# A graph network on one core: low halves of the first node stage computed by GpSimd instead of VectorE

## The chip, the cores and the metric

The kernel runs on one core of one Trainium2 chip. The metric is the time of one execution on the device in microseconds (us). Each run was taken three times; the median is compared. The engines have these names in the profile: PE is TensorE (matmuls), PEld its weight loads, DVE is VectorE, ACT is ScalarE, POOL is GpSimd, SP is SyncE, whose queue here only issues DMAs.

## What is computed

Four graph layers over N = 6250 nodes of 128 features and E = 106250 edges, each followed by a residual and a layernorm:

```python
x = _layernorm(x + _L0_gnn_ref(x, ...))   # relu(relu((x + sum of neighbours) @ W1.T + b1) @ W2.T + b2)
x = _layernorm(x + _L1_gnn_ref(x, ...))   # 4 GCN convolutions: dinv * sum over edges of dinv * h[src], W1..W4
x = _layernorm(x + _L2_gnn_ref(...))      # convolution with edge features
x = _layernorm(x + _L3_gnn_ref(...))      # 2 SAGE convolutions
```

The change concerns the end of the first layer: the layernorm of the first line, and the preparation of its result as operand of the first GCN convolution.

## The kernel before

The sums over neighbours are matmuls with a dense matrix of edge counts ("adjacency"), held in fp8 in HBM. The node features are the stationary operand (128x128, f16). To keep float32 accuracy, each feature block is used as two f16 halves: with a scale c, **high** = f16(c*x) and **low** = f16(c*x - high). Both halves are multiplied with the same adjacency piece and added up in PSUM.

The node features `XN` are 128 partitions x 6272 columns of float32, 49 blocks of 128 nodes. The first node stage goes over them in NQ = 7 chunks (`q` = 0 to 6) of QB = 7 blocks (896 columns). For each chunk:

1. PE: `hidden_0` (L1843), ACT: `relu_0` (L1509), PE: second weight, giving `Y0` in PSUM (L1856).
2. DVE `rows_0(q)`: adds the bias (L1103), takes relu and adds to `XN` (L1105), row statistics (L1108, L1111, L1114).
3. ACT `root_0(q)` (L1515), then DVE `factors_0(q)`: reciprocal (L1119) and the tiny product `c2 = -mean * 1/deviation` (L1121, 128x7, both inputs in SBUF). ScalarE waits for `c2`.
4. ACT `high_0(q)`: normalises `XN` in place, block by block (L1521), then writes the high half `HI[1]` (L1525, tile HN); raises `s_hi`.
5. DVE `low_0(q)`: the low half `LO[1]` (second half of tile HN), seven instructions of 128 columns (L1129), since the scale `c1[:, b]` is one number for each partition and block; raises `s_split`.

DVE runs rows_0(q), factors_0(q-1), low_0(q-2) in that order; ACT runs root_0(q), relu_0(q+2), high_0(q). PE begins the next pass in between: `piece(n)` multiplies seven blocks with two 250-column parts of the adjacency (28 matmuls of 500 columns for a pair of pieces, L1707). Pieces 2j and 2j+1 need the two halves of chunk j, hence `s_split` at NQ + j + 1. Pieces 0 to 7 follow the rows of chunks 3 to 6; pieces 8 to 13 (chunks 4, 5, 6) come behind all rows.

After the stage DVE goes on with `hot(0)` (L1313), the sums of pass 1 (L1203), and the chain `lengths`, `bounds` (L1146 to L773), on which the scales of later passes hang. GpSimd, until then idle, waits for all of `s_split` and adds a bias to `XN` in seven instructions of 896 columns (`bias_1`, L719); that is first read in pass 4. Later it weights edge features (L751).

A tile matters here: `AGN` holds the float32 sums' f16 halves of the input (`HI[0]`, `LO[0]`) until the last sub pass, and is free in the node stage; the first pass writes its results into it.

Of the kernel before, what the change touches and what calls it, by code (L numbers as in the profile page):

```python
# [4 lines left out]
P = 128  # L5


def build(nc, a, out):
# [5 lines left out]
    ALU = mybir.AluOpType  # L14
# [16 lines left out]
    QB = 7  # L31
    NQ = NB // QB
    QN = QB * P
# [86 lines left out]
    with ExitStack() as ctx:  # L120
        def sb(name, shape, dt=fp32):
            return ctx.enter_context(nc.sbuf_tensor(name, shape, dt))

        def sem(name):
            return ctx.enter_context(nc.semaphore(name))

        XN = sb("XN", [P, NP])
        HN = sb("HN", [P, NP])
        HR = sb("HR", [P, NP])
        AGN = sb("AGN", [P, NP])  # L130
# [26 lines left out]
        c1 = sb("c1", [P, NB])  # L157
# [12 lines left out]
        HI = [t[:, 0:NP // 2].bitcast(f16) for t in HL]  # L170
        LO = [t[:, NP // 2:NP].bitcast(f16) for t in HL]
# [178 lines left out]
        s_hi, s_split = sem("high_ready"), sem("split_ready")  # L350
# [280 lines left out]
        def _(pool):  # L631
            g_ = nc.gpsimd
# [64 lines left out]
            def general(p):  # L697
                pool.wait_ge(s_tab, 32 * (PASSES.index(p) + 1))

                def tile(g, j, t, n):  # L700
                    pool.wait_ge(s_stage, NT * PASSES.index(p) + t + 1)
                    pool.sem_inc(s_scrap, 1)
                    g_.indirect_dma_start(out=msg, out_offset=None, in_=Hd[:, :],
                                          in_offset=bass.IndirectOffsetOnAxis(ap=si[:, 0:1], axis=0)).then_inc(s_g[p], 16)
                    g_.indirect_dma_start(out=old, out_offset=None, in_=Gd[:, :],
                                          in_offset=bass.IndirectOffsetOnAxis(ap=di[:, 0:1], axis=0)).then_inc(s_old[p], 16)
                    pool.wait_ge(s_new, NT * PASSES.index(p) + t + 1)
                    pool.sem_inc(s_scrap, 1)
                    g_.indirect_dma_start(out=Gd[:, :], out_offset=bass.IndirectOffsetOnAxis(ap=xi[:, 0:1], axis=0),
                                          in_=new, in_offset=None, bounds_check=NP - 1,  # L710
                                          oob_is_err=False).then_inc(scattered(p, 0)[0], 16)

                tiles(pool, tile)

            def residual_bias(k):

                with pool.Fori(0, NQ) as q:
                    x = XN[:, ds(q * QN, QN)].rearrange("p (b f) -> p b f", f=P)
                    g_.tensor_tensor(x, x, BR[:, k, :].unsqueeze(1).to_broadcast([P, QB, P]), ALU.add)  # L719
                pool.drain().then_inc(s_res, 1)  # L720

            def bias_1():

                pool.wait_ge(s_split, 2 * NQ)
                residual_bias(1)

            def bias_5():

                pool.wait_ge(s_split, splits(5, NU - 1))
                pool.wait_ge(s_tb, idx(5, NU - 1) + 1)  # L730
                residual_bias(5)

            with pool.If(flags["pool"]):
                pool.wait_ge(s_un, NS_)
                g_.memset(at, 0.0)
                g_.affine_select(out=low, in_=ones[:, :], compare_op=ALU.is_gt, fill=0.0, base=0,
                                 pattern=[[-1, P]], channel_multiplier=1)
                pool.drain().then_inc(s_low, 1)
                for p in PASSES:
                    if p == 1:  # L740
                        bias_1()
                    if p == 6:
                        bias_5()
                    general(p)
            with pool.Else():

                def weighted(g):

                    e3 = AE[g % 2].rearrange("p (j f) -> p j f", j=J)
                    pool.wait_ge(s_aem, g + 1)  # L750
                    g_.tensor_tensor(e3, e3, NS[:, g * J:(g + 1) * J].unsqueeze(2).to_broadcast([P, J, DE]), ALU.mult).then_inc(s_aes, 1)  # L751

                bias_1()
                pool.wait_ge(s_ns, 1)
                for g in range(NG):
                    weighted(g)
                bias_5()
        @block.vector
        def _(dve):
            v = nc.vector  # L760
# [314 lines left out]
            with dve.If(flags["dve"]):  # L1075
# [10 lines left out]
                for q in range(NQ):  # L1086
                    cols = slice(q * QN, (q + 1) * QN)
# [11 lines left out]
            def rows_0(q):  # L1099
                cols = slice(q * QN, (q + 1) * QN)  # L1100
                y = Y0[q % 2]
                dve.wait_ge(s_y0, q + 1)
                v.tensor_tensor(three(y), three(y), bias(0, QB), ALU.add)  # L1103
                dve.drain()
                v.scalar_tensor_tensor(out=XN[:, cols], in0=y, scalar=0.0, in1=XN[:, cols], op0=ALU.max, op1=ALU.add).then_inc(s_yb0, 1)  # L1105
                dve.drain()
                for b in range(q * QB, (q + 1) * QB):
                    v.bn_stats(ST[:, b, :], XN[:, b * P:(b + 1) * P])  # L1108
                dve.drain()
                for b in range(q * QB, (q + 1) * QB):  # L1110
                    v.bn_aggr(MV[:, b, :], ST[:, b, :])  # L1111
                dve.drain()
                bs = slice(q * QB, (q + 1) * QB)
                v.tensor_scalar(VE[:, bs], MV[:, bs, 1], EPS, None, ALU.add).then_inc(s_var0, 1)  # L1114
# [6 lines left out]
                v.scalar_tensor_tensor(out=c2[:, bs], in0=MV[:, bs, 0], scalar=-1.0, in1=RS[:, bs],  # L1121
                                       op0=ALU.mult, op1=ALU.mult).then_inc(s_nr0, 1)

            def low_0(q):
                for b in range(q * QB, (q + 1) * QB):
                    cols = slice(b * P, (b + 1) * P)
                    if b == q * QB:
                        dve.wait_ge(s_hi, NQ + q + 1)
                    last = v.scalar_tensor_tensor(out=LO[1][:, cols], in0=XN[:, cols], scalar=c1[:, b:b + 1], in1=HI[1][:, cols],  # L1129
                                                  op0=ALU.mult, op1=ALU.subtract)  # L1130
                last.then_inc(s_split, 1)

            dve.wait_ge(s_aw[0], 16 * len(range(0, NS_, 3)))
            v.tensor_scalar(c1[:, :], dinv[:, :], SC[:, 1, 0:1], None, ALU.mult)
            for q in range(NQ + 2):
                if q < NQ:
                    rows_0(q)
                if 0 < q <= NQ:
                    factors_0(q - 1)
                if q > 1:  # L1140
                    low_0(q - 2)


            def lengths():
# [10 lines left out]
            def bounds():  # L1155
                dve.wait_ge(s_nrt, 1)
                v.scalar_tensor_tensor(out=BND[:, 2:3], in0=NRT[:, 4:5], scalar=LNB, in1=NRT[:, 7:8], op0=ALU.mult, op1=ALU.add)
                v.scalar_tensor_tensor(out=BND[:, 5:6], in0=NRT[:, 3:4], scalar=LNB, in1=BND[:, 5:6], op0=ALU.mult, op1=ALU.add)
                v.tensor_tensor(BND[:, 0:1], NRT[:, 5:6], NRT[:, 6:7], ALU.add)
                dve.drain()  # L1160
                v.scalar_tensor_tensor(out=BND[:, 7:8], in0=BND[:, 0:1], scalar=LNB, in1=BND[:, 7:8], op0=ALU.mult, op1=ALU.add)
                v.scalar_tensor_tensor(out=BND[:, 2:3], in0=BND[:, 2:3], scalar=1.001, in1=NRT[:, 0:1], op0=ALU.mult, op1=ALU.mult)
                dve.drain()
                for p in (2, 5, 7):
                    scale_of(p, BND[:, p:p + 1])
                dve.drain().then_inc(s_scale, 1)
# [212 lines left out]
            with dve.If(flags["dve"]):  # L1379
                for p in range(1, LASTP + 1):  # L1380
                    if p == 1:
                        lengths()
                        bounds()
                    dve.drain()
                    v.tensor_tensor(HR[:, :], HI[p % 2], LO[p % 2], ALU.add)
                    dve.drain()
                    v.tensor_scalar(HR[:, :], HR[:, :], SC[:, p, 1:2], UNIT, ALU.mult, ALU.mult).then_inc(s_gh, 1)
                    if p in (2, 3):
                        for i in (3, 4, 5):
                            measure_steps(p, i)  # L1390
                    general(p)
                    for u in range(NU):
                        general_sums(p, u)
                        rows_read(p, u)
                        if p in LAG["norm"]:
                            normalise(p, u)
                        if p == 4:
                            second(p, u)
                        if p < LASTP:
                            low_half(p, u)  # L1400
            with dve.Else():
                hot(0)
                for n in range(ALL + TAIL):
                    p, i = n // PCS + 1, n % PCS
# [661 lines left out]
```

## Time and profile before

| | |
|---|---|
| median of 3 runs | 2577.36 us (2572.64 to 2578.82) |
| time of the profiled execution | 2576.27 us |
| its span | 2574.4 us, mean granted TensorE clock 0.992 |
| PE busy | 2472.4 us (96%) |
| DVE busy | 1308.8 us (51%) |
| ACT busy | 599.7 us (23%) |
| POOL busy | 162.3 us (6%) |

The rows come from one profiled execution. A timeline row gives the start, the time from the first start to the last end of the merged instructions, engine, line, operation, output and inputs, the count, and in brackets how long the engine was idle before and who ended that. Granted clock is given as a share of 2.4 GHz, so 0.50 is the level of 1.2 GHz. The span leaves 1.87 us of the execution's time outside.

### The profile page before, as it was taken

Reading aid. Unit: us, or ns where it says so; the run is one execution under the profiler, and the core shown is the slowest. Engines: PE = TensorE matmul, PEld = TensorE weight load, DVE = VectorE, ACT = ScalarE, POOL = GpSimd, SP = SyncE. Lnnn points to the kernel's source line nnn. Section 1 sums busy time; section 2 is a strip of 40 time slices with the busy share of each in tenths; the row PEclk is TensorE's granted clock in tenths of the full one; section 3 lists DMA queues with packets and bytes.
Section 4 is the critical chain, followed back from the end, with each engine's and each line's share of the span. In section 5 each row is a group of like instructions: output and inputs, shape, how many; then the busy total and the mean of one; then the engine's idle time right before and its main releaser. Section 6 shows DMA issues by size and latency. Waiting matters only on the chain.

```text
span 2574.4 us, 38685 instructions
## 1 busy us (share of the span) xinstructions
PE 2472.4 (96%) x15714; PEld 1460.8 (57%) x15714; DVE 1308.8 (51%) x3604; ACT 599.7 (23%) x717; POOL 162.3 (6%) x117
## 2 busy tenths in 40 slices
PE   2889999799999999999999999999999999999998
PEld 1768999655555555555555555555555555555545
DVE  7888888457877666676666333332222122122222
ACT  3879999550000111111111000000000000000000
POOL 4000000020000111111111000000000200000000
PEclk8999999999999999999999999999999999999999
DMA  5736222347776666666665565554454554545554
GB/s 164 90 100 90 98 105 105 128 124 225 240 237 199 197 182 187 192 181 185 190 185 173 150 190 140 140 143 135 139 138 124 148 139 135 142 137 148 158 152 109
DMA packets 294912, 395.38 MB, mean 154 GB/s; under 512 B 82249, under 2 KB 282565, under 8 KB 291269
## 3 DMA queue, kind: packets, MB, share of 16 engines
q1 hardware_dynamic: 243960, 326.08, 45.6%
q10 hardware_dynamic: 49964, 64.80, 7.9%
q8 instruction: 126, 2.06, 0.3%
q0 software_dynamic: 800, 1.94, 0.3%
q14 instruction: 62, 0.50, 0.1%
HBM read 343.43 MB, written 49.32 MB: 153 GB/s over the span
## 4 chain that ended last, share of the span: by engine, by line
PE 89%; DVE 3%; DMA 2%; issue 2%; SPq 1%; ACT 1%; DVEq 1%; POOL 1%; ACTq 0%; POOLq 0%
PE PS L1707 82%; PE PS L1891 1%; SPq L530 1%; PE PS L1898 1%; PE PS L1899 1%; DVE TB L962 1%; DMA HR<-adjacency 1%; PE PS L1913 1%; DMA edge_rows<-AT 1%; POOL AT L671 0%; PE PS L1843 0%; PE PS L1896 0%; PE PS L1895 0%; PE PS L1922 0%; PE PS L1871 0%
## 5 line engine op out<-in xcount | busy, mean ns | idle before, releaser
L1707 PE MATMUL PS<-HR,HN 128*128 128x500 fp8e3 (+1 forms) x5096 | 1059.2, 365 | 2.0 <-DVE HN L1129 1.5
L1707 PE MATMUL PS<-HR,AGN 128*128 128x500 fp8e3 (+1 forms) x4606 | 915.1, 349 | 3.4 <-DMA HR<-adjacency 2.1
L1707 PEld LDWEIGHTS PS<-HR,HN 128*128 128x128 f16 x5096 | 488.9, 97 | 517.2 <-issue 3.0
L1707 PEld LDWEIGHTS PS<-HR,AGN 128*128 128x128 f16 x4606 | 445.1, 97 | 400.9 <-issue 4.9
L1707 PE MATMUL PS<-TB 128*128 128x245 f16 x1250 | 319.9, 275 | 28.1 <-DVE TB L962 22.0
L962 DVE TENSOR_TENSOR TB<-HN,HR 128x1240 f16<-128x1240 f16 x250 | 199.9, 800 | 0.0
L1206 DVE SCALAR_TENSOR_TENSOR AT<-PS,SC,TB 128x384 f32<-128x384 f32 (+24 forms) x50 | 21.6, 473 | 324.0 <-PE PS L1707 315.4
L962 DVE TENSOR_TENSOR TB<-iot,HN 128x640 f16<-128x640 f16 x250 | 122.1, 489 | 59.5 <-PE PS L1707 58.7
L1707 PEld LDWEIGHTS PS<-TB 128*128 128x128 f16 x1250 | 122.9, 99 | 51.7 <-DVE TB L962 14.5
L1561 ACT ACTIVATE SD<-VE 128x4 f32<-128x4 f32 (+1 forms) x39 | 8.1, 206 | 596.0 <-DVE VE L1251 596.0
L751 POOL TENSOR_TENSOR AT<-AT,dstI 128x1088 f32<-128x1088 f32 x49 | 100.2, 2045 | 737.3 <-DVE mxe L1332 737.3
L1359 DVE TENSOR_SCALAR TB<-iot,dstF 128x118 f16<-128x118 f16 (+1 forms) x833 | 142.1, 253 | 6.0
L1707 PE MATMUL PS<-HN,AGN 128*128 128x250 fp8e3 x882 | 135.5, 271 | 2.8 <-ACT RBW L1472 2.2
L1493 ACT ACTIVATE HN<-PS 128x980 fp8e3<-128x980 f32 x108 | 128.7, 1229 | 26.9 <-PE PS L1707 19.6
L1707 PE MATMUL PS<-TB,AGN 128*128 128x250 fp8e3 x784 | 124.6, 272 | 3.2 <-DVE TB L976 3.2
L1493 ACT ACTIVATE TB<-PS 128x980 fp8e3<-128x980 f32 x96 | 116.2, 1224 | 15.2 <-PE PS L1707 12.8
L1493 ACT ACTIVATE HR<-PS 128x980 fp8e3<-128x980 f32 x96 | 116.0, 1227 | 14.8 <-PE PS L1707 12.6
L1209 DVE TENSOR_SCALAR AT<-PS,SC 128x384 f32<-128x384 f32 (+24 forms) x50 | 21.6, 473 | 188.7 <-PE PS L1707 181.1
L1623 ACT ACTIVATE AT<-AT,SCE 128x1088 f16<-128x1088 f32 x49 | 58.9, 1202 | 198.3 <-DVEq L1342 140.5
L719 POOL TENSOR_TENSOR XN<-XN,BR 128x896 f32 x14 | 29.0, 2109 | 1089.2 <-ACT TB L1579 594.1
L1707 PEld LDWEIGHTS PS<-HN,AGN 128*128 128x128 f16 x882 | 86.1, 98 | 12.1 <-ACT HR L1493 2.4
L1707 PEld LDWEIGHTS PS<-TB,AGN 128*128 128x128 f16 x784 | 76.6, 98 | 11.0 <-issue 3.5
(249 smaller groups left out, 1708.3 us busy)
## 6 DMA issues: line engine op xcount, KB each, us to landing
HR<-adjacency SPq DMA_DIRECT2D x588, 437.5 KB, 3.5
AT<-source_lanes ACTq DMA_DIRECT2D x49, 544.0 KB, 4.9
AT<-in_edge_attr_dram ACTq DMA_DIRECT2D x144, 128.0 KB, 3.2
adjacency<-HN SPq DMA_DIRECT2D x9, 1531.2 KB, 5.5
adjacency<-HR SPq DMA_DIRECT2D x8, 1531.2 KB, 5.8
adjacency<-TB SPq DMA_DIRECT2D x8, 1531.2 KB, 5.6
HR<-adjacency SPq DMA_DIRECT2D x49, 218.8 KB, 2.5
AT<-in_edge_attr_dram ACTq DMA_DIRECT2D x48, 160.0 KB, 4.2
```

The source lines that it names most:

```text
L530: sp.dma_start(v[0:PTAIL, NG - 1, j0:j0 + w], a[name][e0:e0 + PTAIL * w].rearrange("(p j) -> p j", j=w)).then_inc(s_idx, 16)
L719: g_.tensor_tensor(x, x, BR[:, k, :].unsqueeze(1).to_broadcast([P, QB, P]), ALU.add)
L751: g_.tensor_tensor(e3, e3, NS[:, g * J:(g + 1) * J].unsqueeze(2).to_broadcast([P, J, DE]), ALU.mult).then_inc(s_aes, 1)
L962: last = v.tensor_tensor(rows_[:, :, c0_:c0_ + n].rearrange("p w (c r) -> p w c r", r=REP), row[:, 0:n].rearrange("p (c r) -> p c r", r=RE ...
L1359: v.tensor_scalar(row, iot[:, 0:row.shape[1]], dstF[:, g * J + j:g * J + j + 1], None, ALU.is_equal)
L1493: c.activation(a3[:, i0:i1, :, :], TW[:, b:b + i1 - i0, 0:HC].rearrange("p w (h d) -> p w h d", d=WD), ACT.Copy, scale=UNIT, saturate=Fals ...
L1623: c.activation(AHL[k][:, :, 0:DE], AE[k].rearrange("p (j f) -> p j f", j=J), ACT.Copy, scale=SCE[:, k, 0:1]).then_inc(s_ahi, 1)
L1707: return t_.matmul(out_, w, m, start=start, stop=True, skip_group_check=True)
L1891: last = t_.matmul(y, t_b, WN[:, p, :], start=True, stop=True)
L1898: t_.matmul(y, t_b, WT[:, 2 * p - 10, :], start=True, stop=True)
L1899: last = t_.matmul(Y2[:, b * P:(b + 1) * P], TB[:, node], WT[:, 2 * p - 9, :], start=True, stop=True)
L1913: last = t_.transpose(Z[:, b * P:(b + 1) * P], source, ident[:, :])
```

## The change

`low_0` of VectorE goes. GpSimd gets `lows_0`: for each chunk it waits for the high half, multiplies the whole chunk of `XN` by `c1` (spread along the 128 columns of each block) into `AGN` as float32, drains, and subtracts the high half from it into `LO[1]`. Two instructions of 896 columns stand for seven of 128. `lows_0` runs ahead of `bias_1` on GpSimd, in both branches. VectorE's loop is one turn shorter. In the branch for other graphs (not taken with these inputs) VectorE gets a wait for `s_split`.

```diff
+            def lows_0():
+                for q in range(NQ):
+                    cols = slice(q * QN, (q + 1) * QN)
+                    x, t = (k[:, cols].rearrange("p (b f) -> p b f", f=P) for k in (XN, AGN))
+                    pool.wait_ge(s_hi, NQ + q + 1)
+                    g_.tensor_tensor(t, x, c1[:, q * QB:(q + 1) * QB].unsqueeze(2).to_broadcast([P, QB, P]), ALU.mult)
+                    pool.drain()
+                    g_.tensor_tensor(LO[1][:, cols], AGN[:, cols], HI[1][:, cols], ALU.subtract).then_inc(s_split, 1)
...
+                lows_0()
                 bias_1()
                 pool.wait_ge(s_ns, 1)
...
-            def low_0(q):
-                for b in range(q * QB, (q + 1) * QB):
-                    cols = slice(b * P, (b + 1) * P)
-                    if b == q * QB:
-                        dve.wait_ge(s_hi, NQ + q + 1)
-                    last = v.scalar_tensor_tensor(out=LO[1][:, cols], in0=XN[:, cols], scalar=c1[:, b:b + 1], in1=HI[1][:, cols],
-                                                  op0=ALU.mult, op1=ALU.subtract)
-                last.then_inc(s_split, 1)
-
...
-            for q in range(NQ + 2):
+            for q in range(NQ + 1):
                 if q < NQ:
                     rows_0(q)
-                if 0 < q <= NQ:
+                if q:
                     factors_0(q - 1)
-                if q > 1:
-                    low_0(q - 2)
```

VectorE, from the statistics of one chunk to the rows of the next, before. `c` is the tile c1 or c2, `deviation_0` is raised by ScalarE's root, `high_ready` is `s_hi`:

```order
L1111 BN_AGGR MV<-ST 128x2 x7
L1114 TENSOR_SCALAR VE<-MV 128x7
L1119 RECIPROCAL RS<-SD 128x7 [waits deviation_0]
L1121 SCALAR_TENSOR_TENSOR c<-MV,RS 128x7
L1129 SCALAR_TENSOR_TENSOR HN<-XN,c,HN 128x128 [waits high_ready]
L1129 SCALAR_TENSOR_TENSOR HN<-XN,c,HN 128x128 x6
L1103 TENSOR_TENSOR PS<-PS,BR 128x896 [waits rows_0]
```

The same place after; lines are numbered 12 higher there:

```order
L1123 BN_AGGR MV<-ST 128x2 x7
L1126 TENSOR_SCALAR VE<-MV 128x7
L1131 RECIPROCAL RS<-SD 128x7 [waits deviation_0]
L1133 SCALAR_TENSOR_TENSOR c<-MV,RS 128x7
L1115 TENSOR_TENSOR PS<-PS,BR 128x896 [waits rows_0]
```

The seven narrow instructions and their wait for ScalarE's high half are gone; the tiny product stays where it was.

GpSimd in the branch that is taken, before: bias, then the edge weights (`split_ready` is `s_split`).

```order
L717 UNCONDITIONAL_BRANCH [waits split_ready]
L717 ISA
L719 TENSOR_TENSOR XN<-XN,BR 128x896
L717 REGISTER_ALU
L717 COMPARE_AND_BRANCH
L751 TENSOR_TENSOR AT<-AT,dstI 128x1088 [waits edge_features_measured,source_factors_ready]
```

After, the last two of seven such pairs and the bias behind them:

```order
L728 TENSOR_TENSOR AGN<-XN,c 128x896 [waits high_ready]
L730 TENSOR_TENSOR HN<-AGN,HN 128x896
L728 TENSOR_TENSOR AGN<-XN,c 128x896 [waits high_ready]
L730 TENSOR_TENSOR HN<-AGN,HN 128x896
L717 UNCONDITIONAL_BRANCH [waits split_ready]
L717 ISA
L719 TENSOR_TENSOR XN<-XN,BR 128x896
```

The pairs stand ahead of the bias loop in GpSimd's order; the drain between the two of a pair is not listed.

## Rows read from the trace of the kernel before

**Rows 1.** The page: busy time by engine, and the chain that ended last.

```profile
PE 2472.4 (96%) x15714; PEld 1460.8 (57%) x15714; DVE 1308.8 (51%) x3604; ACT 599.7 (23%) x717; POOL 162.3 (6%) x117
PE 89%; DVE 3%; DMA 2%; issue 2%; SPq 1%; ACT 1%; DVEq 1%; POOL 1%; ACTq 0%; POOLq 0%
```

**Rows 2.** Stretches: length, busy by engine (count), granted clock, DMA share, GB/s.

```profile
505.60:509.00 3.40, 3.36 (x5) 1.72 (x6) 3.16 (x17) 0.00 (x0) 0.00 (x0) 0.51 0.00 0
...
526.00:551.80 25.80, 25.80 (x136) 14.57 (x134) 19.48 (x79) 17.24 (x50) 0.00 (x0) 1.00 0.40 109
...
553.30:571.00 17.70, 17.69 (x84) 8.21 (x85) 5.10 (x18) 9.39 (x29) 6.66 (x4) 1.00 0.59 182
```

**Rows 3.** Timeline of PE in the node stage.

```profile
505.64 3.36 PE L1843 MATMUL PS<-AT,WT 128*128 128x448 f32 x4 [3.02 <-ACT TB L1509]
...
520.35 6.08 PE L1707 MATMUL PS<-HR,HN 128*128 128x500 fp8e3 x28
...
545.77 6.08 PE L1707 MATMUL PS<-HR,HN 128*128 128x500 fp8e3 x28
553.31 17.92 PE L1707 MATMUL PS<-HR,HN 128*128 128x500 fp8e3 x84 [1.46 <-DVE HN L1129]
```

**Rows 4.** Timeline of DVE in the node stage.

```profile
534.42 0.17 DVE L1121 SCALAR_TENSOR_TENSOR c<-MV,RS 128x7 f32<-128x7 f32 x1
...
543.39 0.17 DVE L1121 SCALAR_TENSOR_TENSOR c<-MV,RS 128x7 f32<-128x7 f32 x1
...
545.97 1.10 DVE L1103 TENSOR_TENSOR PS<-PS,BR 128x896 f32<-128x896 f32 x1 [0.58 <-PE PS L1856]
...
551.25 0.17 DVE L1121 SCALAR_TENSOR_TENSOR c<-MV,RS 128x7 f32<-128x7 f32 x1
551.33 1.92 DVE L1129 SCALAR_TENSOR_TENSOR HN<-XN,c,HN 128x128 f16<-128x128 f32 x7
...
556.89 0.17 DVE L1121 SCALAR_TENSOR_TENSOR c<-MV,RS 128x7 f32<-128x7 f32 x1
...
562.14 1.93 DVE L1129 SCALAR_TENSOR_TENSOR HN<-XN,c,HN 128x128 f16<-128x128 f32 x7 [3.25 <-ACT HN L1525]
```

**Rows 5.** Timeline of ACT: the high halves of chunks 2, 4, 5 and 6.

```profile
528.52 2.15 ACT L1525 ACTIVATE HN<-XN,c 128x128 f16<-128x128 f32 x7
...
546.47 2.15 ACT L1525 ACTIVATE HN<-XN,c 128x128 f16<-128x128 f32 x7
...
554.32 2.15 ACT L1525 ACTIVATE HN<-XN,c 128x128 f16<-128x128 f32 x7
...
559.96 2.15 ACT L1525 ACTIVATE HN<-XN,c 128x128 f16<-128x128 f32 x7
```

**Rows 6.** Groups of POOL by form: count, busy us, mean ns, idle before.

```profile
L751 POOL TENSOR_TENSOR AT<-AT,dstI 128x1088 f32<-128x1088 f32 x49 | 100.2, 2045 | 737.3 <-DVE mxe L1332 737.3
L719 POOL TENSOR_TENSOR XN<-XN,BR 128x896 f32 x14 | 29.0, 2109 | 1089.2 <-ACT TB L1579 594.1 <-DVE HN L1129 495.1
...
L693 POOL TENSOR_TENSOR BR<-BR 128x128 f32<-128x128 f32 x1 | 0.8, 819 | 2.1 <-issue 2.1
L662 POOL TENSOR_SCALAR O<-I 128x128 f16<-128x128 f16 x1 | 0.5, 538 | 0.2 <-issue 0.2
L691 POOL TENSOR_TENSOR BR<-BR 128x128 f32<-128x128 f32 x1 | 0.5, 516 | 0.0
```

**Rows 7.** Timelines of DVE and POOL where both were busy, around 1308 us.

```profile
1307.70 0.74 DVE L1297 SCALAR_TENSOR_TENSOR AGN<-TB,SC,AGN 128x512 f16<-128x512 f32 x1
1307.87 2.45 POOL L751 TENSOR_TENSOR AT<-AT,dstI 128x1088 f32<-128x1088 f32 x1 [13.62 <-DVE mxe L1332]
...
1309.13 0.15 DVE L1338 TENSOR_SCALAR mie<-mce 128x1 int32<-128x1 int32 x1
```

**Rows 8.** POOL's timeline at 1131 us.

```profile
1131.31 2.01 POOL L751 TENSOR_TENSOR AT<-AT,dstI 128x1088 f32<-128x1088 f32 x1 [7.69 <-DVE mxe L1332]
```

**Rows 9.** L1359 from 1131 to 1134.4 us: durations min/median/max in ns, starts.

```profile
L1359 DVE TENSOR_SCALAR TB<-iot,dstF x8: 242/243/1072, 1132.3 to 1134.3; 128x118 f16<-128x118 f16 x7, 128x208 f16<-128x208 f16 x1
```

More of the change, by code:

```diff
@@ L751, in weighted @@
                     g_.tensor_tensor(e3, e3, NS[:, g * J:(g + 1) * J].unsqueeze(2).to_broadcast([P, J, DE]), ALU.mult).then_inc(s_aes, 1)
+                lows_0()
                 bias_1()
@@ L1383, in _ @@
                         bounds()
+                        dve.wait_ge(s_split, 2 * NQ)
                     dve.drain()
```

## The prediction

> **What bounds the kernel now.** I read the page first: PE is busy 96% of the span, and the chain that ended last is 89% PE [rows 1]. So the change can matter only where PE waits for a low half, in the node stage (about 491 to 571 us), or where it makes PE wait anew. Next come the timelines of that stage, one engine at a time. PE has no gap from 526 to 551.8 us, at the full clock [rows 2]. It waits for a low half once: at 553.31, idle for 1.46 us, released by L1129 [rows 3]. That is chunk 4, whose high half ScalarE had finished at 546.47 + 2.15 = 548.62 [rows 5], but VectorE came to its low half only at 551.33, behind the rows of chunk 6 that began at 545.97 [rows 4]. From 553.31 the last 84 matmuls (pieces 8 to 13) run back to back, 17.92 us, or 5.97 for the pair of pieces of one chunk [rows 3], up to 571.2.
>
> VectorE is not the bound of the stage: it waits for PE's rows, even ahead of the last chunk (0.58 us idle at 545.97, [rows 4]). The 7 x 1.92 = 13.4 us that leave VectorE are therefore nearly all beside its own waits. What counts is when each low half is ready.
>
> **The change part by part.** Removed: seven times 1.92 us of VectorE. Its rows and statistics keep their times, since PE's rows release them. Nothing but the wait of 1.46 us can be won.
>
> Added: fourteen GpSimd instructions. No row shows this multiply or this subtraction, so I bound them. L719 (896 columns, two inputs) takes 2.11 us on average, L751 (1088 columns, second input spread along the columns as c1 is here) 2.05, L691 (128 columns) 0.52 [rows 6]. From 0.52 and 2.11 at 128 and 896 columns: 2.07 ns a column and some 0.25 us fixed. L751 then has (2.05 - 0.25) / 1088 = 1.65 ns a column, which gives the multiply 0.25 + 896 x 1.65 = 1.73 us. I take 1.7; the bounds are 1.68 (L751 by proportion) and 2.1 (as L719). The subtraction reads and writes f16. As L719 it takes 2.1 us, and this I take. Its upper bound: the one f16 form on GpSimd took 0.54 us for 128 columns [rows 6], 4.2 ns a column, so 3.8 us; below, 1.7. The drain between the two: 0.2 us as in front of L662, or 2.1 as in front of L693 [rows 6]; I take 0.2, since L693 stood behind GpSimd's own DMAs. The pair is thus 1.7 + 0.2 + 2.1 = 4.0 us (3.6 to 8.0), where VectorE took 1.92. GpSimd starts about 0.1 us behind the high half, as it is free.
>
> A second cost: **the two engines block each other.** At 1307.87 L751 took 2.45 us and not 2.01 [rows 7, 8], while VectorE's L1297, with two inputs in SBUF, ran until 1308.44. And an L1359 that began at about 1132.3, while GpSimd was busy from 1131.31 to 1133.32 [rows 8], took 1.07 us against 0.24 [rows 9]: it stood still until GpSimd's instruction was over. A one-column, one-input instruction at 1309.13 ran in its usual 0.15 us beside GpSimd [rows 7]. The Trainium skill (SBUF — State Buffer, "Who interferes with whom") says that a VectorE instruction with two SBUF inputs contends with a GpSimd one that reads SBUF, and that the later one waits for the whole of the other; these rows agree.
>
> L1121 (c2) has two inputs in SBUF, and ScalarE's high half waits for it. So I let it wait for the GpSimd instruction that runs when it comes. The high half lasts 5.0 us from c2 to its end (557.1 to 562.1, [rows 4, 5]). Worked forward:
> - Chunk 2's high half ends at 528.52 + 2.15 = 530.7 [rows 5]. GpSimd's pair: 530.8 to 534.8. c2 of chunk 3, at 534.42 [rows 4], ends at 535.0, 0.4 late. High half of chunk 3 until 540.0.
> - GpSimd's pair until 544.1. c2 of chunk 4, at 543.39 [rows 4], ends at 544.3, 0.7 late. High half until 549.3. The low half of chunk 3 is wanted at 545.77 [rows 3] and is there.
> - Pair of chunk 4: multiply 549.4 to 551.1, subtraction 551.3 to 553.4. c2 of chunk 5 comes at 551.25 [rows 4], in the gap between the two. I take it that it passes; high half until 556.5. PE begins pieces 8 and 9 at 553.4, as before.
> - Pair of chunk 5: multiply 556.6 to 558.3. c2 of chunk 6, at 556.89 [rows 4], waits until 558.3, so the high half of chunk 6 ends at 563.5 and not at 559.96 + 2.15 = 562.1. Low half of chunk 5 at 560.6. PE is done with chunk 4 at 553.4 + 5.97 = 559.4: it waits 1.2 us.
> - Pair of chunk 6: 563.6 to 567.6. PE is done with chunk 5 at 566.6: it waits 1.0 us more, and ends at 573.6.
> Against 571.2 that is **+2.4 us**. For comparison, VectorE's last low half began at 562.14 and was there at 564.07 [rows 4].
>
> Moved: bias_1 (7 x 2.1 us) starts 3.5 us later and ends at about 582.5. Nobody reads it before pass 4. But the tiny products in bounds, two SBUF inputs each, now fall beside it, and its last instruction can hold them up to 1.3 us more; part of it reaches PE through the lookups behind. I take 0.6 of 0 to 1.3. Behind that PE is the bound [rows 1], so a delay stays. Sum: 2.4 + 0.6 = **+3.0 us**, from 2576.27 of the profiled execution to 2579.3. That execution lies 1.1 below the median of the runs shown, so the forecast is 2580 to 2580.5; I say 2580, no measurable change. A measurement of this kernel can tell some 0.3%, 7.7 us, from none.
>
> A page speaks against the edit as such: the Trainium skill (GPSIMD Engine Reference, "Performance versus the Vector engine") gives 4497 ns for a two-input instruction of 2048 columns on GpSimd and 2293 on VectorE. By proportion that is an estimate of 1.97 us for each of the pair, 4.1 with the drain, and the sum would be +3.1 in place of +3.0.
>
> **The rivals.**
> - *No blocking of c2* (15%). For it: it is only seven columns wide, and the 128x1 instruction ran freely [rows 7], though with one input. Then high halves keep their times: low halves at 552.7, 560.6 and 566.2, PE starts 552.8, 560.6, 566.6 and ends 572.5, so +1.3, about 2578.7.
> - *c2 of chunk 5 comes 0.1 us later* (20%), just behind the start of the subtraction, and waits it out. High half of chunk 5 until 558.6, its low half 562.7; c2 of chunk 6 again behind a multiply, low half of chunk 6 at 569.8; PE ends at 575.8. +4.6, with the bounds +5.2, about 2582.5. Against it only that the gap is where I computed it; that is a matter of 0.1 us.
> - *Slower, GpSimd becomes the bound* (9%). If the subtraction takes 3.8 us (f16) and the drain 2.1, the pair is 7.6 us, and chunks come at 562.1 - 548.6 = 13.5 us for the last two [rows 5], 6.7 each. GpSimd then falls behind from the start: the low half of chunk 0 is ready at 522.0 where PE wants it at 520.35 [rows 3], that of chunk 3 at 551.3 against 545.77, that of chunk 6 at 574.4. PE ends at 580.4: +9.2, about 2586.5. It decides from a pair of about 7.3 us. PE's waits would then reach 3 us, and after an idle time of 3.02 us [rows 3] PE ran at 0.51 of the clock [rows 2], its four matmuls in 3.36 us: 1 to 2 us more. Against it: both slow values are needed, and each is from a single odd instruction.
> - *Faster: VectorE's relief counts in full* (3%). 13.4 us less would give 2564. It needs VectorE as the bound, against its wait at 545.97 [rows 4] and PE without a gap [rows 2]. If only the 1.46 us wait were won, this would be inside "the same".
> The forecast itself has 53%.
>
> **How the numbers follow.** Forecast, no blocking, and late c2 are all within 0.3%: 88%. The slower case has 9%, the faster 3%. The range: from the little that could be won (-1.5) with the spread of runs (a median can come out 1 to 2 us lower) to the late c2 and half of the slower case: 2574.5 to 2586.
>
> **What would show it.** GpSimd: L728 near 1.7 us, L730 near 2.1, a gap near 0.2. VectorE: L1133 longer than 0.17 us in chunks 3, 4 and 6, above all 1.4 to 1.6 us in the last. PE: the wait of 1.46 us about the same, and two new ones of 1.0 to 1.2 us ahead of the pieces of chunks 5 and 6, released by POOL; piece 13 ends at 573 to 574. VectorE about 13.4 us less busy. Wrong would be: PE's pieces 0 to 7 waiting for POOL, a pair above 7 us, or PE's last pieces earlier than before.

## The result and the profile after

| | before | after |
|---|---|---|
| median | 2578.5 us (2572.64 to 2582.28, 17 runs) | 2585.26 us (2582.28 to 2589.68, 17 runs) |
| ratio | 1 | 1.0026, 95% interval [1.0019, 1.0033] |
| span of the profiled execution | 2574.4 us | 2586.3 us |

The change costs 0.19 to 0.33%, 5 to 8.5 us. 2585.26 us is inside the range given, 0.7 us below its top, and the ratio itself is within 0.3%. But it is a real loss of about twice the 3 us forecast, and not a null result: with 17 runs of each kernel the interval reaches only 0.07% to either side.

To compare stages free of what varies ahead of them, I use two lengths. The **stretch** runs from PE's first adjacency matmul of the node stage to the end of piece 13 (the start of the matmul that follows, L1863 before and L1865 after). The **part ahead** runs from the first hidden matmul to the beginning of the stretch. In three profiles of each kernel:

| | before | after |
|---|---|---|
| stretch | 50.71, 50.72, 50.73 us | 56.22, 56.04, 56.00 us |
| part ahead | 28.73, 28.66, 28.70 us | 30.18, 30.89, 28.72 us |
| from the stretch to the end of the span | 2003.3 us (first profile) | 2003.7 us (first profile) |

So the stretch holds +5.4 us, within 0.2 us in each profile. Behind it nothing is lost or given back that shows: the second and third profiles have 2005.2 and 2004.9 us there before, 2004.5 and 2003.8 after. The two first profiles lie 11.9 us apart, more than the stretch explains: 4.6 us of it lie ahead of the first hidden matmul (at 491.62 before, at 496.17 after), where both kernels do the same work, 1.5 in the part ahead, 5.5 in the stretch and 0.4 behind.

PE's rows of the changed kernel (first profile), as [rows 3]:

```profile
521.73 3.22 PE L1845 MATMUL PS<-AT,WT 128*128 128x448 f32 x4 [3.62 <-ACT TB L1511]
524.79 1.73 PE L1858 MATMUL PS<-WT,TB 128*128 128x128 f32 x14
526.35 6.08 PE L1709 MATMUL PS<-HR,HN 128*128 128x500 fp8e3 x28
...
551.78 6.08 PE L1709 MATMUL PS<-HR,HN 128*128 128x500 fp8e3 x28
560.21 6.09 PE L1709 MATMUL PS<-HR,HN 128*128 128x500 fp8e3 x28 [2.35 <-POOL HN L730]
569.07 13.66 PE L1709 MATMUL PS<-HR,HN 128*128 128x500 fp8e3 x56 [2.77 <-POOL HN L730]
582.57 1.02 PE L1865 MATMUL PS<-TB,ones 128*128 128x512 f32 x2
```

They show three losses. The wait ahead of piece 8 grew from 1.46 [rows 3] to 2.35 us. A new one of 2.77 us stands ahead of piece 10. And the last 56 matmuls take 13.66 us; at the pace of [rows 3] (84 in 17.92) they would take 11.95. The granted clock explains the last (columns as in [rows 2]):

```profile
566.30:569.07 2.77, 0.00 (x0) 0.00 (x1) 0.71 (x1) 2.02 (x6) 2.57 (x2) 1.00 0.56 158
569.07:572.00 2.93, 2.93 (x8) 1.07 (x9) 0.00 (x0) 2.86 (x10) 0.00 (x0) 0.50 0.04 15
572.00:575.00 3.00, 3.00 (x15) 1.37 (x14) 0.00 (x0) 1.30 (x5) 2.71 (x2) 0.92 0.49 114
```

Behind the wait of 2.77 us PE ran at half the clock (1.2 GHz) for some 3 us: 8 matmuls where 15 fit afterwards. In sum 0.9 + 2.9 + 1.7 = 5.5 us in this profile (2.9: from 560.21 to 569.07 it is 8.86 us, where a pair of pieces takes 5.97).

Why the low halves were late stands on VectorE and GpSimd. VectorE in the changed kernel (L1126 is VE, L1133 is c2; before they were L1114 and L1121, [rows 4]):

```profile
549.47 1.84 DVE L1133 SCALAR_TENSOR_TENSOR c<-MV,RS 128x7 f32<-128x7 f32 x1
...
556.52 1.64 DVE L1126 TENSOR_SCALAR VE<-MV 128x7 f32<-128x7 f32 x1
558.07 0.19 DVE L1131 RECIPROCAL RS<-SD 128x7 f32<-128x7 f32 x1
558.34 1.84 DVE L1133 SCALAR_TENSOR_TENSOR c<-MV,RS 128x7 f32<-128x7 f32 x1
```

GpSimd at the same time:

```profile
547.58 1.68 POOL L728 TENSOR_TENSOR AGN<-XN,c 128x896 f32<-128x896 f32 x1 [5.16 <-ACT HN L1527]
549.41 1.88 POOL L730 TENSOR_TENSOR HN<-AGN,HN 128x896 f16<-128x896 f32 x1
556.45 1.68 POOL L728 TENSOR_TENSOR AGN<-XN,c 128x896 f32<-128x896 f32 x1 [5.16 <-ACT HN L1527]
558.27 1.88 POOL L730 TENSOR_TENSOR HN<-AGN,HN 128x896 f16<-128x896 f32 x1
```

Both VectorE instructions are seven columns wide and take 0.17 us alone. VE at 556.52 is that of chunk 6, c2 at 558.34 that of chunk 5. VE at 556.52 meets the multiply and ends as the multiply ends, at 558.1. c2 at 558.34 meets the subtraction begun at 558.27 and ends as that ends, at 560.2. And since ScalarE's high half waits for c2, GpSimd's next pair starts 5.2 us after the last one ended: from chunk 1 to chunk 5 the engines run in step, 8.87 us a chunk. That costs time from chunk 4 on: before, the high half of chunk 5 came 7.85 us behind that of chunk 4 [rows 5], now 8.86 us. Over the seven chunks, c2 in the changed kernel (durations min/median/max in ns), and the busy times of its page:

```profile
L1133 DVE SCALAR_TENSOR_TENSOR c<-MV,RS x7: 167/1839/1846, 515.3 to 565.6; 128x7 f32<-128x7 f32 x7
PE 2478.1 (96%) x15714; PEld 1463.4 (57%) x15714; DVE 1308.1 (51%) x3555; ACT 599.7 (23%) x717; POOL 187.6 (7%) x131
```

VectorE has 49 instructions fewer, 13.4 us of work, and is busy for only 0.7 us less (1308.8 in [rows 1]), since the profile counts a blocked instruction as busy: the seven c2 took 9.1 us in place of 1.2, the seven VE 4.5 in place of 1.2, and the first `hot` (L1314), now beside `bias_1`, 1.81 in place of 1.04.

The pattern is not the same in each profile. In the second and third, the waits alternate in the earlier chunks: once VE takes 1.83 or 1.90 us and c2 behind it 0.17, otherwise c2 takes 1.59 to 1.85. In all three, VE of chunk 6 takes 1.40 to 1.64 us and c2 of chunk 5 behind it 1.84.

### The profile page after: what moved, and what is told of

The parts are those of the page before. It is cut to its first block, busy times and chain, and to the rows that moved or that the text cites. A ratio compares the mean times of both kernels' runs of the same rounds, so it can differ in the third digit from the quotient of the medians.

```text
span 2586.3 us, 38657 instructions
## 1 busy us (share of the span) xinstructions
PE 2478.1 (96%) x15714; PEld 1463.4 (57%) x15714; DVE 1308.1 (51%) x3555; ACT 599.7 (23%) x717; POOL 187.6 (7%) x131
## 4 chain that ended last, share of the span: by engine, by line
PE 75%; issue 16%; DVE 2%; DMA 2%; SPq 1%; POOL 1%; DVEq 1%; POOLq 1%; ACT 0%; ACTq 0%
PE PS L1709 70%; PE PS L1893 1%; SPq L530 1%; PE PS L1900 1%; PE PS L1901 1%; DMA HR<-adjacency 1%; PE PS L1915 1%; DMA edge_rows<-AT 0%; POOL AT L671 0%; POOL HN L730 0%; PE PS L1898 0%; PE PS L1897 0%; PE PS L1924 0%; DVE TB L974 0%; POOLq L729 0%
## 5 line engine op out<-in xcount | busy, mean ns | idle before, releaser
L1225 DVE TENSOR_TENSOR TB<-PS,dinv 128x512 f32<-128x512 f32 (+1 forms) x39 | 25.8, 660 | 98.8 <-PE PS L1893 98.3
```

What stands on the lines that cost most here:

```text
L1225: v.tensor_tensor(three(temp(p, u)), three(Y[:, 0:n]), spread(dinv, u), ALU.mult).then_inc(s_t, 1)
```

## The experiments

All ratios are to the kernel before, run beside the experiment on the same chip. Lengths of the stretch are from one profile each; the three profiles of either kernel lie up to 0.22 us apart.

### e1_unlock: both tiny instructions made so that they don't collide

```diff
-                v.scalar_tensor_tensor(out=c2[:, bs], in0=MV[:, bs, 0], scalar=-1.0, in1=RS[:, bs],
-                                       op0=ALU.mult, op1=ALU.mult).then_inc(s_nr0, 1)
+                for b in range(q * QB, (q + 1) * QB):
+                    last = v.tensor_scalar(c2[:, b:b + 1], MV[:, b, 0:1], RS[:, b:b + 1], -1.0, ALU.mult, ALU.mult)
+                last.then_inc(s_nr0, 1)
...
-                v.tensor_scalar(VE[:, bs], MV[:, bs, 1], EPS, None, ALU.add).then_inc(s_var0, 1)
...
-                c.activation(SD[:, bs], VE[:, bs], ACT.Sqrt).then_inc(s_sd0, 1)
+                c.activation(SD[:, bs], MV[:, bs, 1], ACT.Sqrt, bias=eps[:, 0:1]).then_inc(s_sd0, 1)
```

> The changed kernel, with both tiny VectorE instructions of the stage made so that GpSimd should not block them: VE is left out (ScalarE's root takes the variance and adds eps itself, as bias), and c2 is made by seven one-column instructions with one tensor input. GpSimd's pairs stay as they are. Measure: the stretch from PE's first adjacency matmul of pass 1 to the end of piece 13, 50.9 us before, 56.4 after. Theory A (blocking makes the high halves late): the high halves come as before, a low half only by the longer pair later: stretch 52.0 (51.5 to 52.7), about 4 to 5 us faster than the changed kernel, waits of PE about 0.6, 1.9 and 0. Rival B (the pair of 3.75 us in place of 1.92 is the cost by itself): stretch stays at 56 or more.

The edit also takes out a drain of VectorE ahead of VE. Measured: stretch 52.90 us. PE's waits, then VectorE beside GpSimd instructions that run:

```profile
554.30 6.09 PE L1710 MATMUL PS<-HR,HN 128*128 128x500 fp8e3 x28 [1.11 <-POOL HN L732]
561.78 6.08 PE L1710 MATMUL PS<-HR,HN 128*128 128x500 fp8e3 x28 [1.39 <-POOL HN L732]
568.66 6.09 PE L1710 MATMUL PS<-HR,HN 128*128 128x500 fp8e3 x28 [0.79 <-POOL HN L732]
```

```profile
550.55 1.68 POOL L730 TENSOR_TENSOR AGN<-XN,c 128x896 f32<-128x896 f32 x1 [5.28 <-ACT HN L1528]
551.70 0.17 DVE L1131 RECIPROCAL RS<-SD 128x7 f32<-128x7 f32 x1
551.95 0.94 DVE L1134 TENSOR_SCALAR c<-MV,RS 128x1 f32<-128x1 f32 x7
558.83 0.94 DVE L1134 TENSOR_SCALAR c<-MV,RS 128x1 f32<-128x1 f32 x7 [0.45 <-issue]
```

With GpSimd's fourteen instructions unchanged, 3.2 of the 5.4 us are gone, as theory A has it. I put the remaining 2.2 us down to the longer pair and the 0.94 us of the seven narrow products; no run measures the two apart. My 52.0 left the products out, so the value missed its band (51.5 to 52.7) by 0.2. PE's waits came out at 1.11, 1.39 and 0.79 us where I expected 0.6, 1.9 and 0. The run's ratio, 1.0020 [1.0010, 1.0029] (2583.69 against 2578.1 us), is no measurable gain over the changed kernel; I had expected 4 to 5 us, so that part failed. Its part ahead was 31.94 us in the profile, 3.2 more than before, which would hide what the stretch gained: three bursts of PE took 3.35, 3.15 and 3.09 us there where they took 1.77, 1.86 and 2.20 before, and the slower c2 delays ScalarE. As a remedy the edit is worth nothing; as a test of the mechanism the stretch decides.

### e2_c2_narrow and e3_no_ve: c2 alone, VE alone

The two halves of the diff above, one at a time.

> The changed kernel with c2 alone made by seven one-column instructions; VE stays a 7-column instruction with one input. Theory A with c2 as the main victim: stretch 52 to 53, VE still waits up to 1.6 us for GpSimd's multiply. If VE's wait weighs as much as c2's: 54 to 55. Rival B: 56.

Measured: stretch 53.18 us, just above the band of 52 to 53, ratio 1.0022 [1.0012, 1.0032]. PE's waits were 1.38, 1.88 and 0.33 us, each with matmuls at the full clock behind it.

> The changed kernel with VE alone left out (the root adds eps); c2 stays one 7-column instruction with two SBUF inputs. Theory A: c2 is reached earlier, in or before the multiply, and waits for it or for the subtraction: stretch 53 to 55.5, between e1 and the changed kernel. If only VE mattered: 52. Rival B: 56.

Measured: stretch 53.98 us, ratio 1.0018 [1.0008, 1.0027]. c2 still waits, and PE behind it:

```profile
551.84 1.55 DVE L1133 SCALAR_TENSOR_TENSOR c<-MV,RS 128x7 f32<-128x7 f32 x1
558.96 1.28 DVE L1133 SCALAR_TENSOR_TENSOR c<-MV,RS 128x7 f32<-128x7 f32 x1
```

```profile
553.43 6.09 PE L1709 MATMUL PS<-HR,HN 128*128 128x500 fp8e3 x28 [0.33 <-POOL HN L732]
562.29 13.44 PE L1709 MATMUL PS<-HR,HN 128*128 128x500 fp8e3 x56 [2.78 <-POOL HN L732]
```

Either edit breaks the step in which the engines run: of 56.1 us, 2.9 come back from c2, 2.1 from VE, 3.2 from both. They are not additive. I read it so: VE's wait is what puts c2 on the subtraction, so without VE c2 waits for less. The clock has a part in it too, which these runs don't separate: in e3 a wait of 2.78 us again had half the clock behind it, 13.44 us for 56 matmuls (1.5 more than 11.95), in e1 and e2 none did.

### e6_fill: PE's waits filled with scrap work

```diff
+                if n in (8, 10):
+                    for k in range(11):
+                        mm(X0[0], HI[1][:, 0:P], HI[1][:, 0:UN], start=True)
```

> The changed kernel with 11 scrap matmuls of 448 columns (about 0.19 us each) on PE ahead of pieces 8 and of 10, in PE's two new waits, nothing else changed. Theory C (PE's idle time of 2.8 us drops its clock to 1.2 GHz for some 3 us, which costs 1.5 us on top of the waits): the clock stays at 1.00 behind the second wait, stretch 54.9, the run 1 to 2 us faster. Rival: the drop has another cause: stretch 56.4 or more, since the scrap work can only delay.

Measured: stretch 55.37 us, ratio 1.0023 [1.0014, 1.0031].

```profile
559.09 2.24 PE L1709 MATMUL PS<-HN 128*128 128x448 f16 x11
562.04 6.09 PE L1709 MATMUL PS<-HR,HN 128*128 128x500 fp8e3 x28 [0.71 <-POOL HN L730]
568.90 6.09 PE L1709 MATMUL PS<-HR,HN 128*128 128x500 fp8e3 x28 [0.77 <-POOL HN L730]
```

The pieces start at the same points, but at the full clock (6.09 us a pair). So it was the idle time that had lowered it. The stretch came between my 54.9 and the rival's 56.4: only 0.7 us come back and not 1.5, since PE then reaches the low half of chunk 6 before it is ready (0.77 us of wait, new). At half clock the changed kernel had hidden that wait. The run as a whole, 1 to 2 us faster by my expectation, moved less than its interval.

### e4_split: the last two chunks back on VectorE

```diff
             def lows_0():
-                for q in range(NQ):
+                for q in range(5):
...
+                if q > 1 and q - 2 >= 5:
+                    low_0(q - 2)
```

`low_0` is that of before, with a wait for the low half of the chunk ahead.

> The changed kernel with the low halves of the last two chunks (5 and 6) given back to VectorE's seven narrow instructions; GpSimd makes chunks 0 to 4. Theory A (blocking): the high half of chunk 5 is still late, since c2 waits for GpSimd's pair of chunk 4, but c2 of chunk 6 takes 0.17 us again and both low halves come 1.9 us behind their high halves: stretch 52.7 us (50.7 before, 56.2 changed), PE's idle time stays under 2 us and its clock at 1.00. Rival B (only the pair's length): 51.5 or less, as chunks 5 and 6 have no pair.

Measured: stretch 53.03 us, ratio 1.0006 [0.9996, 1.0016].

```profile
555.08 1.84 DVE L1133 SCALAR_TENSOR_TENSOR c<-MV,RS 128x7 f32<-128x7 f32 x1
562.39 0.17 DVE L1133 SCALAR_TENSOR_TENSOR c<-MV,RS 128x7 f32<-128x7 f32 x1
```

```profile
556.95 6.09 PE L1721 MATMUL PS<-HR,HN 128*128 128x500 fp8e3 x28 [2.15 <-POOL HN L730]
564.49 12.00 PE L1721 MATMUL PS<-HR,HN 128*128 128x500 fp8e3 x56 [1.45 <-DVE HN L1142]
```

c2 of chunk 5 waits for the pair of chunk 4; c2 of chunk 6 finds no pair and takes 0.17 us. 3 us of the loss are gone. The 2.3 left come from the five chunks that GpSimd still makes: PE's wait for chunk 4 is 2.15 us in place of 1.46, and a new one of 1.45 stands ahead of chunk 5. VectorE makes that low half itself; it is late because its high half waited for c2.

### e8_wide_dve: the two wide instructions, on VectorE

```diff
+                x, t = (k[:, cols].rearrange("p (b f) -> p b f", f=P) for k in (XN, AGN))
+                v.tensor_tensor(t, x, c1[:, q * QB:(q + 1) * QB].unsqueeze(2).to_broadcast([P, QB, P]), ALU.mult)
+                dve.drain()
+                v.tensor_tensor(LO[1][:, cols], AGN[:, cols], HI[1][:, cols], ALU.subtract).then_inc(s_split, 1)
```

> The kernel before with the low half made by the same two wide instructions (multiply into AGN, drain, subtract), but on VectorE. If the engine is what costs and not the split in two: two of 1.1 us and a drain, 2.3 us in place of 1.92, stretch 51.1 us, run within 1 us of before. Rival (going through AGN as float32 costs by itself): stretch above 53.

Measured: stretch 50.66 us, ratio 1.0001 [0.9992, 1.0010]. Two of 1.08 and 1.09 us in place of seven: the form costs nothing in the stretch. Moving it to the other engine does.

### e7_scrap_pairs: GpSimd's pairs as scrap, the low halves on VectorE

```diff
+            def dummies():
+                for q in range(NQ):
...
+                    pool.wait_ge(s_hi, NQ + q + 1)
+                    g_.tensor_tensor(t, x, c1[:, q * QB:(q + 1) * QB].unsqueeze(2).to_broadcast([P, QB, P]), ALU.mult)
+                    pool.drain()
+                    g_.tensor_tensor(AGN[:, cols].bitcast(f16)[:, 0:QN], AGN[:, cols], HI[1][:, cols], ALU.subtract).then_inc(s_dum, 1)
```

> The kernel before, with all low halves on VectorE, and GpSimd doing the same fourteen instructions at the same moments as in the changed kernel, but as scrap into AGN, which no later step of the stage reads (ScalarE waits for the last pair before it computes its squares). PE waits for none of them. Theory A (blocking): VE, c2 and now also the narrow low halves (two SBUF inputs) wait for GpSimd: c2 up to 1.8 us, stretch 55 to 59 us though each low half is VectorE's. Rival B (the cost is that PE waits for a pair of 3.7 us): stretch 50.7 as before.

Measured: stretch 56.63 us, ratio 1.0022 [1.0012, 1.0032]. PE now waits for VectorE:

```profile
548.64 6.08 PE L1719 MATMUL PS<-HR,HN 128*128 128x500 fp8e3 x28 [1.07 <-DVE HN L1140]
557.50 7.77 PE L1719 MATMUL PS<-HR,HN 128*128 128x500 fp8e3 x28 [2.77 <-DVE HN L1140]
```

```profile
553.78 1.83 DVE L1132 SCALAR_TENSOR_TENSOR c<-MV,RS 128x7 f32<-128x7 f32 x1
...
562.37 3.54 DVE L1140 SCALAR_TENSOR_TENSOR HN<-XN,c,HN 128x128 f16<-128x128 f32 x7
567.55 5.08 DVE L1140 SCALAR_TENSOR_TENSOR HN<-XN,c,HN 128x128 f16<-128x128 f32 x7 [1.63 <-ACT HN L1536]
```

PE waits for no result of GpSimd, and yet the stretch is as long as in the changed kernel. So rival B is out as the whole cause: blocking alone can cost that much. The run doesn't tell how the changed kernel's 5.4 us divide, since here the narrow low halves are blocked as well, which the changed kernel no longer has on VectorE: 1.92 us by themselves, they stretch to 3.54 and 5.08 us beside a pair. For the division there is only e1: 3.2 us without the blocking of VE and c2, 2.2 left.

### e9_reorder: PE's wait attacked without GpSimd

```diff
-            def rows_0(q):
+            def rows_0(q, between=lambda: None):
...
+                between()
...
+                if q == NQ - 1:
+                    rows_0(q, lambda: (low_0(NQ - 3), factors_0(NQ - 2)))
```

> The kernel before with nothing on GpSimd; on VectorE the low half of chunk 4 and the factors of chunk 5 are moved into the rows of chunk 6, between the residual (L1105) and the statistics. This aims at PE's wait of 1.46 us without GpSimd. Low half of chunk 4 ready 30.2 us into the stretch in place of 32.9, PE's wait for it gone, that for chunk 5's low half new with 0.7 us: stretch 49.9 to 50.2, 0.5 to 0.8 us less than before, 0.03% of the run, no measurable difference in the median. If VectorE were the bound of the stage, the stretch would not move or grow.

Measured: stretch 49.96 us, median 2577.81 against 2578.99 us, ratio 0.999 [0.9982, 0.9999].

```profile
546.34 1.93 DVE L1130 SCALAR_TENSOR_TENSOR HN<-XN,c,HN 128x128 f16<-128x128 f32 x7 [0.40 <-ACT HN L1528]
548.46 0.17 DVE L1122 SCALAR_TENSOR_TENSOR c<-MV,RS 128x7 f32<-128x7 f32 x1
```

```profile
543.46 11.99 PE L1710 MATMUL PS<-HR,HN 128*128 128x500 fp8e3 x56
556.17 12.00 PE L1710 MATMUL PS<-HR,HN 128*128 128x500 fp8e3 x56 [0.71 <-DVE HN L1130]
```

The one wait that the change could have removed is gone, by an order on VectorE; one of 0.71 us for chunk 5 takes its place. The gain of 0.8 us in the stretch is as expected. The ratio is the lowest here, but its interval ends just below 1, and 1.2 us between the medians is more than the stretch gives, so of a faster run I claim no more than the 0.8 us.

### More profiles of both kernels

> The kernel before once more, for a second profile. The stretch should be 50.7 us again (within 0.3). Open is the part ahead of it: from the first hidden matmul to the first piece 28.7 us in the first profile, 30.2 in the changed kernel; if the clock's level there is chance, it may come out at 28.7 or at 30.2 to 31.

> The changed kernel once more, for a second profile and its time beside the experiments. Stretch 56.2 us again; the part ahead of it 28.7 to 31. If blocking sets the times, VE and c2 of chunk 5 wait again for the multiply and the subtraction of chunk 4.

> The kernel before, a third profile, for the part ahead of the stretch. In the profiles so far PE's second burst of hidden matmuls (4, after 1.25 us idle) took 1.77 us in before, before_again, e8_wide_dve and e6_fill, and 3.35 in the changed kernel twice and in e1 to e4. If that is chance, some profile of this kernel shows 3.35; if it goes with the kernel, this one shows 1.77 again. Stretch 50.7.

> The changed kernel, a third profile, for the same question: 3.35 us again if it goes with the kernel, 1.77 possible if it is chance. Stretch 56.1.

The stretches and parts ahead are in the table above. VE and c2 waited again around chunk 5: 1.43 and 1.84 us in the second profile. The changed kernel, timed again: 2584.65 against 2579.93 us, 1.0018 [1.0009, 1.0026]. The stretch's 5.4 us are 0.21% and lie in both intervals. The third profile of the changed kernel:

```profile
493.58 3.35 PE L1845 MATMUL PS<-AT,WT 128*128 128x448 f32 x4 [5.33 <-issue]
498.18 1.77 PE L1845 MATMUL PS<-AT,WT 128*128 128x448 f32 x4 [1.25 <-ACT TB L1511]
```

It shows the fast second burst, so the slow one (3.35 us, in two of its three profiles) is not a fixed property of the change. Of the fourteen profiles, five of five without GpSimd instructions in the stage are fast there, and two of nine with them. So the odds may well depend on the kernel. How they could stays open: GpSimd's first instruction in the stage comes 20 us later (520.62 against 500.77), and no experiment was made on it. The part ahead is 1.5 and 2.2 us longer in the two profiles of the changed kernel that have the slow burst.

## Why the prediction was right, and where it failed

The time fell inside the range, and "within 0.3%" came out. Part of that is luck: the top of the range, 2586, was there for a slower GpSimd, which did not come, and the median is 0.7 us below it.

**Right: what bounds the stage.** VectorE's relief (13.4 us of work) bought nothing, and PE without a gap up to piece 7 stayed so. The waits that count are those for chunks 4 and 5.

**Right: the durations.** Multiply 1.69 us (1.7 taken), subtraction 1.88 (2.1 taken; f16 did not slow it), gap 0.15 (0.2 taken). The slow rival, a pair of 7.3 us or more, was far away.

**Right: blocking of c2**, with both inputs in SBUF: up to 1.84 us in place of 0.17. The rule of the Trainium skill (SBUF — State Buffer, "Who interferes with whom") that an instruction with two SBUF inputs contends with GpSimd agrees with this trace; e1, where c2 had one tensor input and one column, ran beside GpSimd in 0.94 us whether a pair was running or not, but it changed input and width together.

**Wrong: "c2 of chunk 5 comes at 551.25, in the gap between the two. I take it that it passes."** It came 0.07 us behind the start of the subtraction and took 1.84 us. This was the rival with 20%, which I had called a matter of 0.1 us. It isn't: the prediction has no wait for VE, which has one input and seven columns and is blocked as well. It took 1.64 us, until the multiply was over, and so was released just when the subtraction was about to begin, with c2 0.2 us behind its end (558.16 and 558.34). All three profiles show the same for this chunk, so it did not hang on 0.1 us.

The rows to see it were there. I had read the wait of L1359 [rows 8, 9] as an agreement with the rule on two inputs. But L1359 reads one tensor, `iot`; `dstF` is its scalar, one number for each partition. It is the same kind of instruction as VE, TENSOR_SCALAR with one tensor input, and it stood still until GpSimd was done. The same section of the Trainium skill counts this kind among those that can use both ports. The prediction let a one-column instruction that ran freely [rows 7] stand for VE. Width alone does not decide either: RECIPROCAL, with one input and seven columns too, took its 0.17 us beside the multiply in e1 (at 551.70). One-column instructions with one tensor input never waited here, but no run varies the width of VE alone.

The price of that rival was +4.6 us. With the clock kept up, in e6, the stretch was 4.65 us longer than before. That the two agree so well is partly luck, since the rival was priced with a pair of 4.0 us and it took 3.7.

**Wrong in size: the high halves' delay.** Taken as 0.7 us for chunk 4; relative to the start of the stretch it was 1.8 (556.37 - 526.35 = 30.0 against 548.62 - 520.35 = 28.3). So the first wait grew by 0.9 us where I had 0, and the second was 2.8 us where I had 1.2.

**Missing: the clock.** I had the row of a 3.02 us idle time with half clock behind it [rows 2, 3], and used it only for the slow rival. Half the clock came behind 2.77 us too, and the last 56 matmuls took 1.7 us more. e6 gave back 0.7 of it, the rest went into the wait for chunk 6.

**Wrong: the wait for chunk 6.** 1.0 us forecast, none seen, since PE was too slow to reach it; e6 brings it out with 0.77.

**Wrong: VectorE's busy time.** 13.4 us less were forecast, 0.7 less came; waits beside GpSimd in c2, VE and the first `hot` make up 12.0 of the difference.

**Not there: the 0.6 us in bounds.** The first of those products came at 590.70, as the last bias instruction was ending (590.89), and took 0.21 us and not 0.16; the rest came behind it.

In numbers: 2.4 + 0.6 = 3.0 forecast; 0.9 + 2.9 + 1.7 = 5.5 measured in the stretch of the first profile, 5.4 over three. The rest of the medians' 6.8 us (their interval begins at 5) can be noise or the burst ahead; which of them was not shown.

## What to carry to other kernels

Before work goes from VectorE to GpSimd, list what stays on VectorE while it runs, tiny instructions above all: a 0.17 us instruction on the path can wait for the whole of a wide GpSimd instruction, and if another engine's next step starts from it and in turn releases GpSimd, a collision can come back in every round. Look for the wait that ends last, here 1.46 us for one chunk, and ask whether an order on the same engine removes it. And price each new idle time of PE with the clock: behind 2.77 us here 56 matmuls took 1.7 us more, of which 0.7 us was the net loss.

## What was not expected of the hardware

- A VectorE instruction of seven float32 columns with one SBUF input (VE) took 1.64 us in place of 0.17 beside GpSimd; one-column ones with one tensor input (e1, and [rows 7]) never did, and neither did RECIPROCAL with seven columns (e1, 0.17 us).
- GpSimd's 896 columns took 1.69 us with an operand repeated along the columns, 1.88 us with float32 and f16 in and f16 out, against 2.11 on average for L719 [rows 6].
- Ahead of the pieces of this stage, PE's clock stayed at 1.00 behind idle times of 2.10 to 2.35 us (the changed kernel and e4, four profiles) and was at half behind each of 2.77 and 2.78 us (the changed kernel, e3 and e7, five profiles).
